# Layers 0, 1 and 2 of the next graph moved into layer 3's ring of the current one

## What is computed

```
x = layernorm(x + gat0(x, adj))     # 1 head: e[i,j] = leaky(s_src[i] + s_dst[j]), masked softmax over j, attn @ h, elu
x = layernorm(x + gat1(x, adj))     # the same with other weights and a bias
x = layernorm(x + mha2(x, adj))     # 8 heads: leaky(q k^T / 8 + edge_bias[edge]), masked softmax, attn @ v, projection
x = layernorm(x + gat3(x, adj))     # e[i,j] = sum_f a[f] * leaky(u[i,f] + v[j,f]), masked softmax over j, attn @ hp, elu
```

## Time and profile before

| what | us |
|---|---|
| median of 2 runs (8804.68 and 8809.75) | 8807.22 |
| span of the profiled execution | 8820.9 |
| PE busy | 7888.1 (89%) |
| DVE busy | 7363.6 (83%) |
| ACT busy | 7107.8 (81%) |
| PE weight loads busy | 3520.0 (40%) |
| POOL busy | 1432.9 (16%) |

### The profile page before, as it was taken

How to read it: one execution, slowest core, us unless ns; L and a number is a source line. 1 busy time by engine, 2 the same in 40 slices (tenths; PEclk the granted TensorE clock), 3 DMA queues, 4 the chain that set the end, 5 groups by cost and what they waited for, 6 DMA issues and landing times.

```text
span 8820.9 us, 165559 instructions
## 1 busy us (share of the span) xinstructions
PE 7888.1 (89%) x57857; PEld 3520.0 (40%) x58440; DVE 7363.6 (83%) x11117; ACT 7107.8 (81%) x8295; POOL 1432.9 (16%) x582
## 2 busy tenths in 40 slices
PE   3898998989989899898989989899898998989999
PEld 2434435344353433434334343343534435344342
DVE  3788887988879888798888988888788887988888
ACT  2788787977879788797887978879797786977878
POOL 0301204021040310303012030120402104021000
PEclk7999999999999999999999999999999999999999
DMA  2614426144261532516235171442614426153250
GB/s 69 166 37 104 114 54 160 42 120 96 58 151 49 136 75 72 139 49 156 50 90 127 45 175 34 102 116 56 160 40 115 103 53 155 47 129 82 61 126 19
DMA packets 430043, 822.72 MB, mean 93 GB/s; under 512 B 163874, under 2 KB 221218, under 8 KB 427042
## 3 DMA queue, kind: packets, MB, share of 16 engines
q1 hardware_dynamic: 429090, 810.76, 38.1%
HBM read 76.25 MB, written 4.19 MB: 9 GB/s over the span
## 4 chain that ended last, share of the span: by engine, by line
PE 31%; issue 27%; SPq 18%; ACT 16%; DVE 5%; POOL 2%; DMA 1%; ACTq 0%; DVEq 0%; POOLq 0%
PE psum L881 18%; SPq L437 18%; ACT work L1108 11%; PE psum L663 2%; ACT spare L950 2%; PE psum L585 2%; ACT spare L945 2%; PE psum L580 1%; PE psum L758 1%; PE psum L599 1%; DVE work L1331 1%; PE psum L848 1%; DVE work L1492 1%; PE psum L733 1%; PE psum L771 1%
## 5 line engine op out<-in xcount | busy, mean ns | idle before, releaser
L881 PE MATMUL psum<-work,pick 128*32 128x512 f32 x32768 | 3750.9, 598 | 116.9 <-ACT work L1108 58.3
L1108 ACT ACTIVATE work<-spare,ucol 128x1024 f32<-128x1024 f32 x3477 | 3702.4, 1142 | 13.3 <-PE psum L881 10.1
L1492 DVE TENSOR_SCALAR work<-spare,ucol 128x1024 f32<-128x1024 f32 x4715 | 3204.2, 745 | 72.1 <-PE psum L881 53.8
L881 PEld LDWEIGHTS psum<-work,pick 128*32 128x32 f32 x32768 | 979.7, 110 | 2439.1 <-issue 2059.4
L1018 ACT ACTIVATE work<-psum,beta 128x1024 f32<-128x1024 f32 x1024 | 1140.0, 1113 | 549.8 <-PE psum L733 397.6
L1359 DVE STREAM_TRANSPOSE work<-work 128x1024 f32<-128x1024 f32 x960 | 1191.0, 1241 | 263.7 <-DMA work<-work 203.0
L1331 DVE CUSTOM_DVE_ANT_0 work<-psum,work 128x1024 f32<-128x1024 f32 x1024 | 1225.2, 1197 | 176.8 <-ACT work L1018 168.3
L1025 ACT ACTIVATE work<-work,least 128x1024 f32<-128x1024 f32 x1024 | 1173.0, 1145 | 19.6 <-DVE least L1331 19.6
L1575 POOL TENSOR_TENSOR rstd<-rstd,neg_half 128x8 f32<-128x8 f32 x64 | 131.7, 2057 | 5198.1 <-DVE rstd L1269 5198.1
L733 PE MATMUL psum<-x_split,q_hi 128*128 128x512 f32 x2048 | 860.3, 502 | 0.0
L729 PE MATMUL psum<-mask,ident_b 128*128 128x512 bf16 x1793 | 587.6, 399 | 299.8 <-DVE least L1331 272.3
(11 more groups left out here) (179 smaller groups left out, 7072.4 us busy)
## 6 DMA issues: line engine op xcount, KB each, us to landing
work<-work SPq DMA_DIRECT2D x2560, 128.0 KB, 2.4
spare<-work SPq DMA_DIRECT2D x1280, 128.0 KB, 2.6
adj_in<-in_adj SPq DMA_DIRECT2D x128, 512.0 KB, 5.1
q_lo<-adj_in SPq DMA_DIRECT2D x1024, 64.0 KB, 2.0
q_lo<-spare SPq DMA_DIRECT2D x1024, 64.0 KB, 2.0
work<-work SPq DMA_DIRECT2D x1792, 32.0 KB, 1.8
mask<-mask_next SPq DMA_DIRECT2D x16, 2048.0 KB, 9.2
x_in<-in_x SPq DMA_DIRECT2D x16, 256.0 KB, 9.7
```

What stands on the lines that cost most here:

```text
L881: mm = pe.matmul(slot[32 * q:32 * q + 32, cols], pick[:, 15 - kk:47 - kk], ring[kk % 4][q][:, cols], start=False, stop=(kk == 15), skip_gr ...
L1108: ins = act.activation(ring[kk % 4][q], v3, ACT.Relu, bias=ucol[:, 4 * T + q, kk:kk + 1])
L1492: ins = dve.tensor_scalar(ring[kk % 4][q], v3, ucol[:, 4 * T + q, kk:kk + 1], 0.0, ALU.add, ALU.max)
```

## The change

Layer 2 of graph g+1 joins layers 0 and 1 inside the ring of graph g. A ring is now 160 slots. In each slot there is a ring step, except at every second tile of layer 2 (32 slots). A slot may hold one score tile of the next graph: layer 0's 8 tiles in slots 6 to 13, layer 1's in 36 to 43, layer 2's 64 in slots 66 to 135 with a gap of 2 slots after each 16. ACT's and DVE's parts of a tile follow 2 slots behind PE's (`ACT_LAG`, `DVE_LAG`), the exponential 3, the transposition 4.

Layer 3 has one score buffer (`score3`) in place of two; its mask is added by DVE when it takes the extreme (`top_tile3`), not by PE. The PSUM that this sets free makes two `turn` buffers, used in turn, through which all tiles of layers 0 to 2 now go. The ring holds 3 steps in place of 4, the probabilities 3 buffers in place of 4. All of layers 0 to 2 moves in pairs: 8 pairs for layers 0 and 1 and 32 pairs for layer 2, all tiles included, and layer 3 moves all 8 tiles: 48 moves per graph. A pair has two buffers on either side (`blocks`, `pairT`). The mask is copied in 8 DMAs, one per row block. The 16 matmuls that kept PE busy ahead of the ring (`KEEP`, L848) are gone, as are `turn_tile` and `pv_last`.

```diff
-TILES2 = H * NT
-STEPS2 = HP * NT
-QUADS = STEPS2 // 2
-MOVED = QUADS - 1
-LAG = 5
+TILES_A = 2 * NT
+TILES = TILES_A + H * NT
+PAIRS = TILES // 2
...
+RING = 3
+BASE = (6, 36)
+BASE_2 = 66
+GAP = 2
+ACT_LAG, DVE_LAG = 2, 2
...
+            at[slot + 7 + late] = (k, 0)
+            at[slot + 8 + late] = (k, 1)
...
+MOVE_AT = {slot_of(2 * k + 1) + DVE_LAG + 2: k for k in range(PAIRS)}
...
-        score = [banks(0), banks(2)]
-        turn = banks(4)
+        score3 = banks(0)
+        turns = [banks(2), banks(4)]
...
-        blocks = [quad_of(8), quad_of(12)]
-        quadT = [quad_of(4), quad_of(16), spare[:]]
+        blocks = [two_of(15), two_of(17)]
+        pairT = [two_of(19), two_of(21)]
...
-                for k in range(MOVED):
-                    ready(s_blocks, g * 4 * MOVED + 4 * k + 4)
-                    if k >= 3:
-                        ready(s_pv, g * QUADS + k - 2)
...
-                    move(dst, blocks[k % 2], s_moved[k % 4])
+            def move_pair(a, k):
+
+                ready(s_blocks, a * TILES + 2 * k + 2)
+                if k >= 2:
+                    ready(s_pv, a * PAIRS + k - 1)
+                elif not_first(a):
+                    ready(s_pv, a * PAIRS)
+                move(pairT[k % 2].rearrange("p (i y) -> p i y", i=4), blocks[k % 2], s_moved[k % 8])
...
+            def layer3(g, it, tail, more, loads_on):
+                for s in range(SLOTS):
+                    T, kk = of_step(s)
+                    if kk == 4 and T and more:
+                        copy_mask(g + 1, T - 1)
...
+                    if kk == 6 and T and T > 1:
+                        move_tile(g, T - 1, it, ("pv3", T - 2))
...
+                    if more:
+                        ahead(g + 1, s, loads_on)
...
+            def layer3(g, it, tail, more):
+                it3[0] = it
+                for s in range(SLOTS):
+                    T, kk = of_step(s)
+                    if kk is not None:
+                        ring_step(g, 16 * T + kk)
...
+                    if more:
+                        ahead(g + 1, it, s)
...
-                link(dve.tensor_reduce(top3_max[:], score[T % 2], AX.X, ALU.max))
+                dve.tensor_tensor_reduce(probs3[:], score3, mask[:, T, :], -1.0, 3.0e38, ALU.add, ALU.min,
+                                         top3[:]).then_inc(s_top3, 1)
...
+            def tiles(a, it, s, flagged):
+                if s - DVE_LAG - 2 in TILE_AT:
+                    blocks_of(a, TILE_AT[s - DVE_LAG - 2])
+                if s - DVE_LAG in TILE_AT:
+                    leaky(a, it, TILE_AT[s - DVE_LAG], flagged)
```

More of the change, by code:

```diff
@@ L1117, in _, with column_3 @@
[L1117 to L1125 removed]
+            def column_3(it):
+                filled(act, it, ("column3", 0))
+                act.activation(column3[:], place(it, ("column3", 0)), ACT.Copy).then_inc(s_column3_hi, 1)
```

1747 lines of the change are left out of this document (859 added, 888 removed).

## The result

The changed kernel takes 11,788.7 us (median of two runs, 11,778.5 to 11,798.9) against 8,807.2: 1.338 times as long, 95% interval 1.333 to 1.342, slower by a third. Its profiled execution spans 11,776.7 us, 0.1% under the median. The prediction was 11,150 with a range of 10,350 to 12,150.

What follows compares the result with a forecast made beforehand. No engine alone bounded the kernel before; in layer 2 a cycle through SP's issue would. A graph 409 + 248 + 26 = 683 us; 642 + 15 x 683 + 263 = 11,150 us, range 10,350 to 12,150.

Steps and rivals of the forecast that it cites:

- What bounds the kernel: Whole kernel before: no engine alone decides; ACT and DVE 93% busy in the ring, slack in layer 2 and hand-over.
- the count of moves: SP's queue: 40 pairs and 8 tiles make 48 moves, 509 us of issue per graph, against 30 moves and 318 before.
- Price of a move: SP's queue: issuing one move of 16 DMAs, with waits between groups, takes 10.6 us whether DMAs carry 64 or 128 KB.
- Pace in layer 2: Layer 2's pairs: issue, landing, DVE, PE and hand-overs sum to 23.3 us per two moves; 11.9 taken, bounds 10.6 and 14.9.
- Rival A: Layer 2: SP alone sets the pace at 10.6 us a pair, a graph 641 us, 10,508 in all; chance 0.24.
- The stretch of layer 2: Layer 2's moves, first issue to last landing: 31 x 11.9, three layer 3 tiles and the last landing, 409 us a graph.
- Rest of the ring and layers 0 and 1: Outside layer 2's stretch: 248 us for the rest of the ring and 26 for layers 0 and 1, per graph.
- Work of PE, ACT and DVE: The three engines' own work: no change counted, 0 us, bounds -10 and +10 us per graph.
- The ring with three steps: Ring buffers, 3 steps in place of 4: costs nothing while ACT and DVE are the slower side.
- Ends: First graph without a ring 642 us, last ring and its tail 263 us.
- Rival B: Layer 2: PE's clock falls in most of it, pace 13.5 us, a graph 734, 11,953 in all; chance 0.17.
- Rival C: Moves: issue is hidden and busy work decides, engines at 93%, 8053 us, from a move under 6.9 us; chance 0.03.

Runs made afterwards that it cites:

- n8_moves: Changed kernel with 8 DMAs per move in place of 16, same bytes, VectorE's transposition reading every fourth key: 11,013 us against 11,789.
- n4_moves: Changed kernel with 4 DMAs per move in place of 16, same bytes, VectorE's transposition reading every fourth key: 10,549 us against 11,789.
- units_first: Changed kernel, still 16 DMAs per move, with VectorE's ring units put before the transposition in each slot: 11,455 us, 334 less.
- before_one_score: Kernel before, with PE's first ring step of a tile waiting until VectorE has read the previous tile's scores, read at ring step 1: 9,041 us against 8,840.
- before_ring3: Kernel before, with VectorE and ScalarE allowed only three ring steps ahead of PE: 8,829 us against 8,840.
- fill: Changed kernel with two more zero-weight matmuls on PE ahead of ring steps in layer 2's slots, 34 steps a graph: 11,938 us, 149 more.
- before_n4: Kernel before with 4 DMAs per move in place of 16: 8,828 us against 8,835.
- ring4_n4: Changed kernel with 4 DMAs per move, keys reordered once a graph, ring units before the transposition, four ring steps, layer 3's mask left out: 9,597 us.

## Why the prediction was right, and where it was off

*What bounds the kernel; the count of moves.* Right. 10,240 issues for pairs and 2,048 for tiles are 48 moves a graph, and SP's share in the chain doubled. That it is the number of DMAs and not their bytes alone is shown by n8_moves and n4_moves, which move the same bytes; the time that one DMA takes of SP grows with its size, though, so the number is not all either.

*Price of a move, 10.6 us.* Right: 10.7 (128 us for 12).

*Pace in layer 2, a cycle of 23.3 us over two pairs, taken as 11.9 each.* Right, 12.0, and two legs are shown singly: issue with landing by the runs on the number of DMAs, ring units behind the transposition by units_first. That the sum came out so close is partly luck. Followed through the trace, one cycle (the move issued at 1637.6 to the one issued at 1662.0) takes 24.4 us where the forecast had 23.3: 11.4 for issue and landing (forecast 11.9), 4.1 for VectorE (4.3), but 8.9 for PE (6.5 and hand-overs). Its ring step, at the lower clock, is 3.64 in place of 1.78, and at that place, a gap between two groups of tiles, PE makes q and a second ring step in place of score tiles. In the stretch shown SP had to wait in four of six such cycles. Rival A, SP alone at 10.6, was not far, since SP waits only 1.3 us a move; but under it units_first should have changed nothing, and it brought 334 us. The gaps of VectorE were longer and more than I said: 2,470 us in 502 waits are 4.9 us at 31 pairs a graph, in place of 4 us at 24. PE is busy 68%, not 55 to 60%: at a clock of 0.85 the same work takes longer.

*The stretch of layer 2*: 421 against 409. The clock's part of these 12 us is not taken apart.

*Rest of the ring and layers 0 and 1*: 304 us against 274. This is the step that was off most, and in it the term "Work of PE, ACT and DVE: 0" with bounds of 10 us a graph. It counted work alone. One score buffer adds no work, but it takes overlap away on both sides: PE can't start a tile while VectorE reads the last one, and VectorE, which has to read at once, waits for PE. before_one_score measures it by itself, 1.8 us a turn, and with six turns a graph in this part it is some 11 of the 30 us. The estimate is rough: in the changed kernel itself half of PE's 257.4 us of waiting for this reading stands inside layer 2's stretch. The rings that run without a next graph show it too; first the kernel before, then the changed one, both 128 steps and no move of a pair:

```profile
8558.00:8799.00 241.00, 239.82 (x2184) 73.48 (x2190) 221.72 (x320) 224.13 (x220) 0.00 (x0) 0.99 0.06 17
```

```profile
11481.00:11745.00 264.00, 249.14 (x2252) 77.70 (x2244) 234.21 (x358) 232.93 (x235) 2.01 (x1) 0.99 0.07 19
```

264 in place of 241 us, at the same clock. This ring holds the tail of the graph before as well (VectorE 12.5 us more, ScalarE and PE 9), for which the forecast had a place in the rest of the ring, but none at the end. The moves of layers 0 and 1 took somewhat longer than reckoned. Four of layer 1 are issued in 44.8 us and have landed after 46.4; those of layer 0 take 50 us to the last landing (mean of 15 graphs). The forecast had 44 for each with landing, so 8 us a graph come from here:

```profile
2196.01 44.75 SPq L529 DMA_DIRECT2D work<-work  x64
```

The 11 us that remain of the 30 are not taken apart by any run; the clock outside layer 2, 0.95 where the ring before had 0.99, is the only trace of them that I found. Slots there took 304 / 86 = 3.5 us, not 2.5 to 3.

*The ring with three steps costs nothing.* Right (before_ring3).

*Ends*: 901 against 905, but from two errors: the first graph 605 (642 forecast), the last ring 296 (263), of which 23 are those of the lone ring above.

*Rival B, a fallen clock, 11,953.* The time lies nearer to it than to the forecast, and yet it isn't B: the clock in layer 2 was 0.85, not under 0.8, the pace 12.0, not 13.5, and fill, which raised the clock, did not shorten the stretch. The clock is not free all the same: PE's ring matmuls, the same in number, are busy 4,344 us where they were 3,751, and the part of this that stands in the cycle was not measured by itself.

*Rival C, the issue hidden.* The Trainium skill, "DMA: Bandwidth & Descriptors", section "Issuing engines are not separate DMA queues", has the sequencer's time small beside the DMA. The traces disagree for the moves of this kernel: at 64 KB 16 DMAs take 10.1 us to issue and the last lands 1.6 us later; at 256 KB four take 4.1 us and the last lands 3.3 us later. Rival C was to decide from a move under 6.9 us. With 4.1 us it should have, and its time of 8,053, for engines at 93%, was still not reached: the new schedule took 9,739 with the best order, and 9,597 with four ring steps.

## What to carry to other kernels

When work that uses few buffers is packed closer, follow one buffer around its cycle and add up what every engine does in it, in program order; in the new place each leg is paid, while a share of the chain in the old one (18% for SP) is no price: in before_n4 half of SP's issuing went and nothing was gained. On an engine that works in order, put what waits for nothing ahead of what waits for a transfer, and cut a transfer into few large DMAs when their issue is a leg. Add up the whole group when you read what issue costs, not the median of one DMA. A second buffer that is given up needs a price even if no engine has more to do: here 1.8 us at each of its turns.

## What the runs showed that was not expected

- A 128x1024 f32 transposition on VectorE takes 1.24 us when it reads 32 keys in a row and 2.06 when it reads every fourth.
- The median of a DMA's issue on SP hardly changes from 64 KB (0.59 us) to 128 and 256 KB (0.61), but the groups do not shrink with their number: 1 MB takes 10.1 us in 16 DMAs (13.6 with 8 rows of four pieces each), 6.6 in 8 and 4.1 in 4. Landing goes from 2.0 over 3.7 to 4.6 us after a DMA's own issue. Four DMAs of 512 KB take 7.7 us.
- Beside GpSimd's conversions single units of VectorE take up to 1.9 us longer (2.656 against a median of 0.748), which shows in the mean (0.791) and not in the median; nine tenths of this goes when the conversions are cut short (0.750).
- One ring step of lead less (before_ring3) or more (ring4_n4) is worth 0 to 1.5%, though the waits of the units for PE fall to a fifth and less.
